# Raw weights of the second and third expert fetched one stage earlier, in a fused four-layer kernel

## The reference

```python
x = layernorm(x + dilated_attention(x))        # 16 heads, segments of 256, every second row
x = layernorm(x + expert_layer(x))             # below
x = layernorm(x + linear_attention(x, W))
x = layernorm(x + soft_moe(x, phi, W, b))

# expert_layer, x as 4096 rows of 256
route = softmax(x @ router_w + router_b)
for e in range(8):
    a, g = split(x @ w1[e])                    # w1[e]: 256 x 2048
    y = (silu(a) * g) @ w2[e]                  # w2[e]: 1024 x 256
    out = where(argmax(route) == e, y, out)
out = out * max(route)
```

## Time and profile before

| | us |
|---|---|
| median of 3 runs | 1556.09 (1555.97 to 1556.95) |
| the profiled execution | 1556.61 |
| its span, first to last instruction | 1554.6 |
| TensorE busy in the span | 1387.7 (89%) |
| VectorE, ScalarE, POOL busy | 885.5, 611.6, 672.0 |

### The profile page before, as it was taken

The page is one execution under the profiler, slowest core; times in us unless marked ns, Lnnn a source line. Parts: engine busy times, 40 slices in busy tenths (PEclk is TensorE's granted clock), DMA queues, the critical chain, the costliest instruction groups (busy, mean ns, idle before and its releaser), DMA issues. The chain is left out here.

```text
span 1554.6 us, 27807 instructions
## 1 busy us (share of the span) xinstructions
PE 1387.7 (89%) x8930; PEld 1206.6 (78%) x8931; DVE 885.5 (57%) x1771; ACT 611.6 (39%) x1076; POOL 672.0 (43%) x542
## 2 busy tenths in 40 slices
PE   6997397999999993799969999999999968999997
PEld 3444276888888882577769999999999958989997
DVE  4788522222222223367578787787787734565555
ACT  3554332333333332476543332332332315555553
POOL 6663087776660005211017665565565523150400
PEclk9998688999999996799989999999999988999999
DMA  4112333222220005300032265365366367355440
GB/s 156 45 44 87 111 121 103 95 96 105 96 81 13 13 14 203 95 1 1 1 118 85 82 176 154 102 175 167 93 182 169 92 177 281 127 213 203 149 149 27
DMA packets 109178, 171.17 MB, mean 110 GB/s; under 512 B 6112, under 2 KB 95072, under 8 KB 101696
## 3 DMA queue, kind: packets, MB, share of 16 engines
q1 hardware_dynamic: 100096, 156.00, 31.2%
q0 software_dynamic: 3408, 9.31, 2.1%
q10 hardware_dynamic: 5616, 5.11, 1.0%
HBM read 114.96 MB, written 55.44 MB: 110 GB/s over the span
## 5 line engine op out<-in xcount | busy, mean ns | idle before, releaser
L1492 PE MATMUL disp_psS<-disp_e,last_x 128*128 128x256 f32 x1024 | 233.1, 381 | 3.8 <-POOL disp_e L1575 3.8
L1492 PEld LDWEIGHTS disp_psS<-disp_e,last_x 128*128 128x128 f32 x1024 | 191.1, 191 | 28.5 <-POOL disp_e L1575 4.4
L1582 POOL TENSOR_TENSOR disp_s<-disp_e 128x512 f32<-128x512 f32 x64 | 82.3, 1286 | 262.9 <-ACT disp_e L1562 262.9
L1761 PE MATMUL comb_psO<-comb_yh,comb_eh 128*128 (+1 forms) x512 | 156.6, 306 | 15.3 <-DVE comb_el L1852 11.6
L1544 ACT ACTIVATE disp_raw<-disp_psL 128x512 f32<-128x512 f32 x128 | 76.4, 597 | 220.5 <-PE disp_psL L1477 155.7
L1477 PE MATMUL disp_psL<-phi_hi,disp_xh 128*128 (+1 forms) x512 | 156.9, 306 | 4.9 <-DVE disp_e L1638 4.8
L1575 POOL TENSOR_TENSOR disp_e<-disp_e,disp_rs 128x1024 f32<-128x1024 f32 x64 | 151.7, 2371 | 0.0
L1852 DVE TENSOR_TENSOR comb_el<-comb_psT,comb_eh 128x512 fp32r<-128x512 f32 x128 | 86.7, 687 | 106.4 <-ACT comb_eh L1797 106.4
L1477 PE MATMUL disp_psL<-phi_hi,disp_xl 128*128 (+1 forms) x512 | 145.6, 284 | 0.0
L1477 PE MATMUL disp_psL<-phi_lo,disp_xh 128*128 (+1 forms) x512 | 145.6, 284 | 0.0
L1761 PE MATMUL comb_psO<-comb_yl,comb_eh 128*128 (+1 forms) x512 | 145.5, 284 | 0.0
(11 more groups left out here) (261 smaller groups left out, 3437.1 us busy)
## 6 DMA issues: line engine op xcount, KB each, us to landing
logits<-disp_raw SPq DMA_DIRECT2D x64, 512.0 KB, 4.1
comb_e<-logits SPq DMA_DIRECT2D x32, 1024.0 KB, 4.9
w_raw<-in_w SPq DMA_DIRECT2D x8, 2048.0 KB
disp_wt<-in_w_slot SPq DMA_DIRECT2D x16, 1024.0 KB, 8.1
w_raw<-in_w SPq DMA_DIRECT2D x8, 1024.0 KB
disp_bt<-in_b_slot SPq DMA_DIRECT2D x8, 1024.0 KB, 11.3
comb_y_in<-slot_y SPq DMA_DIRECT2D x4, 2048.0 KB, 10.4
slot_y<-disp_yb SPq DMA_DIRECT2D x60, 128.0 KB, 2.8
```

Of the source, the lines that this page charges most:

```text
L1492: last = nc.tensor.matmul(psS[kd][:, b, :], x[:, b * TB + mc, kd * P:(kd + 1) * P], e[mc % 4][:, b, :], start=mc == 0 and b % 2 == 0, stop ...
L1582: nc.gpsimd.tensor_tensor(s2[:], e[mc % 4][:, 0:2, :], e[mc % 4][:, 2:4, :], ALU.add).then_inc(pair_sum, 1)
L1761: last = nc.tensor.matmul(psO[j % 2][:, 0:D], ep[s % EB][:, i, :], yp[:, bass.ds(odd, 1), ch * D:(ch + 1) * D].rearrange("p a d -> p (a d) ...
```

## The change

Expert 1's raw weights get a place of their own, `next1` and `next2`. It is not new memory: it lies over the second place of `lo1` and `lo2`, which is filled first by expert 1's own low part. `low_chunk` therefore reads a chunk and writes its low part to the same bytes. SP loads expert 1 in the attention, after the loads of segments 2 and 3, once expert 0 has landed. The second pair of segments is written out ahead of the loop, which now begins at 2. In the routing SP loads expert 2 into `raw1` and `raw2`, which are free since expert 0 has been split. In the experts SP's loads begin with expert 3, and its wait for eight gathers is gone.

```diff
--- before.py
+++ after.py
@@ -72,6 +72,10 @@
 
     def sb(self, name, shape, dt=F32):
         return self.ctx.enter_context(self.nc.sbuf_tensor(f"{self.tag}_{name}", shape, dt))
+
+    def over(self, name, shape, offset):
+
+        return self.nc.alloc_sbuf_tensor_at(f"{self.tag}_{name}", shape, F32, offset=offset)
 
     def ps(self, name, shape, dt=F32):
         return self.ctx.enter_context(self.nc.psum_tensor(f"{self.tag}_{name}", shape, dt))
@@ -213,13 +217,15 @@
                 wait(sp, loaded, i * 16)
                 sp.dma_start(dst[:, bass.ds(segs[0], 2), :], src[:, bass.ds(segs[0], 2), :]).then_inc(loaded, 16)
                 for q in range(2):
-                    if not isinstance(i, int):
+                    if not isinstance(i, int) or i > 0:
                         sp.wait_ge(xT_raw, i * 2 + (q - 1))
                     sp.dma_start(xe[q][:], src[:, bass.ds(segs[q], 1), 0:D].rearrange("p a d -> p (a d)")).then_inc(even_loaded[q], 16)
 
             load(0, (0, 1))
             weights.load(sp, 0)
-            with sp.Fori(1, NSEG // 2) as i:
+            load(1, (2, 3))
+            weights.load(sp, 1)
+            with sp.Fori(2, NSEG // 2) as i:
                 load(i, (sp.snap(i * 2), sp.snap(i * 2 + 1)))
 
         @block.gpsimd
@@ -558,7 +564,7 @@
             sp.wait_ge(rw_clear, 1)
             sp.dma_start(rw[:, :, 0:NE], router_w.rearrange("(k p) e -> p k e", p=P)).then_inc(w_loaded, 16)
             sp.dma_start(rb[:], router_b.partition_broadcast(P)).then_inc(w_loaded, 16)
-            weights.load(sp, 1)
+            weights.load(sp, 2)
             for b in range(B):
                 sp.wait_ge(kept, (b + 1) * TB)
                 sp.dma_start(x1_dram.rearrange("(t p) d -> p t d", p=P)[:, b * TB:(b + 1) * TB, :],
@@ -741,9 +747,13 @@
         self.raw1 = m.sb("raw1", [P, KD, 2 * FF])
         self.raw2 = m.sb("raw2", [P, FK, D])
         self.hi1 = m.sb("hi1", [P, 2, KD * 2 * FF], F32R)
+        lo1_at = nc.sbuf_base
         self.lo1 = m.sb("lo1", [P, 2, KD * 2 * FF], F32R)
         self.hi2 = m.sb("hi2", [P, 2, FK * D], F32R)
+        lo2_at = nc.sbuf_base
         self.lo2 = m.sb("lo2", [P, 2, FK * D], F32R)
+        self.next1 = m.over("next1", [P, KD, 2 * FF], lo1_at + 4 * KD * 2 * FF)
+        self.next2 = m.over("next2", [P, FK, D], lo2_at + 4 * FK * D)
         self.zero = m.sb("zero", [P, 1])
         self.loaded1, self.loaded2, self.zeroed = m.sem("loaded1"), m.sem("loaded2"), m.sem("zeroed")
 
@@ -751,9 +761,14 @@
 
     def load(self, sp, e):
 
-        wait(sp, self.split, 4 * e)
-        sp.dma_start(self.raw1[:], self.w1_dram[e].rearrange("(k p) f -> p k f", p=P)).then_inc(self.loaded1, 16)
-        sp.dma_start(self.raw2[:], self.w2_dram[e].rearrange("(k p) d -> p k d", p=P)).then_inc(self.loaded2, 16)
+        raw1, raw2 = (self.next1, self.next2) if e == 1 else (self.raw1, self.raw2)
+        if e in (1, 2):
+            sp.wait_ge(self.loaded1, 16 * e)
+            sp.wait_ge(self.loaded2, 16 * e)
+        if e > 1:
+            sp.wait_ge(self.split, 4 if e == 2 else 4 * e)
+        sp.dma_start(raw1[:], self.w1_dram[e].rearrange("(k p) f -> p k f", p=P)).then_inc(self.loaded1, 16)
+        sp.dma_start(raw2[:], self.w2_dram[e].rearrange("(k p) d -> p k d", p=P)).then_inc(self.loaded2, 16)
 
     def high_slice(self, act, seg, ready):
 
@@ -778,7 +793,7 @@
 
     def divide_high(self, act, e):
 
-        for loaded, raw, hi, _ in self.parts():
+        for (loaded, _, hi, _), raw in zip(self.parts(), (self.next1, self.next2)):
             act.wait_ge(loaded, 16 * (e + 1))
             self.nc.scalar.activation(hi[:, e, :], raw[:].rearrange("p k f -> p (k f)"), ACT.Copy).then_inc(self.high, 1)
 
@@ -789,7 +804,8 @@
 
         first = KD * 2 * FF // self.CHUNK
         part, at = (0, n) if n < first else (1, n - first)
-        _, raw, hi, lo = self.parts()[part]
+        _, _, hi, lo = self.parts()[part]
+        raw = (self.next1, self.next2)[part]
         cols = slice(at * self.CHUNK, (at + 1) * self.CHUNK)
         pool.wait_ge(self.high, 2 * (e - 1) + part + 1)
         last = self.nc.gpsimd.tensor_tensor(lo[:, e, cols], raw[:].rearrange("p k f -> p (k f)")[:, cols], hi[:, e, cols].bitcast(F32),
@@ -858,9 +874,7 @@
 
         @block.sync
         def _(sp):
-            for q in range(4):
-                sp.wait_ge(gathered[q], 32)
-            for e in range(2, NE):
+            for e in range(3, NE):
                 w.load(sp, e)
 
         @block.gpsimd
```

## The result

The changed kernel takes 1568.4 us (median; 1564.37 to 1572.17), the kernel before 1556.32 us, ten runs each: ratio 1.0073, 95% interval [1.0056, 1.0091]. It is 12.1 us slower; a gain of 5.3 us was forecast. The profiled execution is 1566.82 us, its span 1565.0.

What follows compares the result with a forecast made beforehand. One chain of stages bounds the kernel, with TensorE setting the end of the experts. Hole -5.3, attention 0 and routing 0 sum to -5.3 us: 1551.3 us profiled, 1550.8 us median, range 1542 to 1559.5.

Steps and rivals of the forecast that it cites:

- Attention and routing at nothing: Stages before the experts: the moved loads of experts 1 and 2 cost 0 us; attention 2.8 us if transfers took twice as long.
- POOL's two waits go, last gather at 252: Experts: waits of 3.47 and 2.40 us before two gathers vanish, 5.3 us net; last gather at 252.1 instead of 257.34.
- The division starts at 254.1: Experts: POOL's division of expert 2 starts at 254.1 instead of 259.35 us, worth nothing by itself.
- The failed step: Experts: TensorE's slow stretch still begins at 248.07 but ends with the gathers, shrinking from 13.3 to 8.0 us.
- the hole: Experts, kernel before: TensorE's matmuls crawl without a releaser from 248 to about 261.3 us, costing 12.5 us in one tile.
- The other half of the step: Experts: TensorE's slow stretch ends when the last gathered rows land, at about 255.9 us after the change.
- the term of -5.3 us: Experts: the gain from shortening the hole, the only nonzero term; shorter hole given 0.34.
- The prediction's own sign of being wrong: Experts: wrong if the slow stretch keeps 13 us, is absent, starts before 245, or TensorE waits for a split.
- The rival "Slower": Experts: a long unbroken run of gathers makes the hole, then 232.8 to 256 us; 1566 us, chance 0.20.
- the +10: Experts: the slower rival's added cost, a hole of 23.3 us instead of 13.3.
- a late supply of instructions to TensorE: Experts: rival's cause; without the transfer of 223.22 the hole goes, 13.1 us gained, 1543.0 us, chance 0.24.

Runs made afterwards that it cites:

- e3: Changed kernel with expert 2's 3 MB transferred once more at 223 us, its division waiting for the repeat: 1554.1 us, 0.9996 of the kernel before.
- e8: Kernel before, 15 expert gathers in a row, the other 24 one at a time between POOL's divisions of experts 2 to 7: 1539.29 us, ratio 0.989.
- e1: Changed kernel, 15 expert gathers in a row, the other 24 one at a time between POOL's divisions of experts 2 to 7: 1537.17 us, ratio 0.9878.
- e2: Kernel before with expert 2's load held until all 39 gathers have landed: 1566.35 us, ratio 1.0075.
- e13: Changed kernel with a 1.3 us POOL subtraction after the 23rd and 31st expert gather alone: 1560.25 us, 1.0031 of the kernel before.
- e5: Changed kernel with a 128x512 POOL subtraction after each expert gather from the sixteenth on: 1569.03 us, 1.008 of the kernel before.
- e15: Changed kernel with 24 expert gathers placed singly between POOL's divisions, the kernel of e1 run again: 1540.75 us, 0.9907 of the kernel before.
- e12: The changed kernel itself, run again unaltered on one chip with three variants: 1565.97 us, 1.0072 of the kernel before.
- e9: Kernel of e1 plus a POOL subtraction after each linear-attention gather from the ninth on: 1548.65 us, 1.0117 of the kernel before.
- e11: Changed kernel with a 128x512 POOL subtraction after the 23rd and 31st expert gather alone: 1526.68 us, 0.998 of the kernel before.

## Why the prediction was wrong

**Attention and routing at nothing: right.** The routing begins at 143.40 us (143.41 before), and e3, with both early loads and the old transfer, takes the time of the kernel before (0.9996); e8 against e1 agrees.

**POOL's two waits go, last gather at 252: right**, to 0.3 us.

**The division starts at 254.1: wrong by 2.4 us**; it waited for TensorE's signal of the fourth tile, which came with the end of the stream. Nobody waited for it.

**The failed step is the onset of the hole.** The prediction says that it begins "at a place of TensorE's program which the change leaves where it is, at 248.07". It begins some 10 us after the gathers start to come every 1.25 us, wherever TensorE then is: at 232.9 instead of 248.5 us, in another tile and among other matmuls. e3 brought the brake back and the late hole with it, e2 took the brake from the kernel before and got the early one. The other half of the step, that it ends when the gathers have landed, held (255.5 and 256.5 us). With the wrong onset the term of -5.3 us had the wrong sign; measured it is +14.0: the change took away the transfer that had kept half of the hole shut. The prediction's own sign of being wrong, a slow stretch that starts before 245, is what the profile shows.

**The rival "Slower" was right** in place and size: 232.8 to 256 us forecast, 232.9 to 256.5 seen, 1566 against 1568.4 us. Its mechanism was right in that the run of gathers makes the hole; that the run must be unbroken is what e13 refutes, and the +10 was too small by 4 us: it did not have TensorE's wait of 15.15 us for VectorE, which itself waited for a late signal. I gave it 0.20 because TensorE ran evenly in the earlier run of gathers and in the loaded stretch. Both have an answer that stood in the rows: from 190 to 223 us a chunk of POOL work stands between two gathers (2.4 us apart), and up to 238 us the transfer slowed them. In both stretches they were not dense, and the loaded one was not wholly undisturbed: ScalarE's "remote" waits of 2.54 us before 229.12 and 4.20 before 237.45 lie in it. "Nothing else marks the onset" should have weighed more than "TensorE's place did not change", which was no evidence at all: a place in the program explains a slow stretch only if something there is slow.

**What the prediction left out:** the waits of other engines in the hole. ScalarE's "remote" waits in the trace of before would have shown that TensorE's signals are late as well, which a late supply of instructions to TensorE does not explain, and the same waits in the linear attention would have shown a second place with dense gathers and the same sign.

**Open:** by what path gathers hold up TensorE; whether their rate counts or the number in flight; and why one batch of runs does not show it. There the changed kernel itself was not run.

## What to carry to other kernels

Before a transfer is moved away, ask what it slowed down: a brake on another queue can be worth more than the bandwidth it takes. When an engine crawls without a releaser, list what starts about then and what ends with it on every other engine, and weigh the onset as much as the end. Try indirect gathers from GpSimd spaced to 1.6 to 2 us each (by waiting for the second one before, or by putting them between long POOL operations) rather than issued back to back, watch who waits for the last of them (e5 lost 25.1 us there), and time it on more than one chip.

## What the runs showed of the hardware that was not expected

- Gathers of 128 rows issued from GpSimd every 1.25 us delay TensorE: its semaphore increments are 4 us late 9 us after they begin and up to 26 us later on, and from some 10 us on its instructions come 0.7 us or more apart. At 1.35 us on the mean four fifths of it remain, at 1.6 us in the experts and 1.99 us in the linear attention nothing; half the bytes change nothing. The Trainium skill, "SBUF — State Buffer", section Who interferes with whom, holds that a DMA never contends with a compute engine. Taken for the time of a kernel, the measurement says otherwise for these gathers (e15 against e12, on one chip: 25.2 us); no run shows whether SBUF has a part in it.
- The cost is not always there: in one batch of three kernels (e9 to e11), on a chip where nothing else was run, the traces show neither the hole nor the waits, and the kernel before ran in 1529.94 us instead of 1555 to 1556. The four other batches of experiments, on three chips, all had it.
- A POOL subtraction with two inputs from SBUF stretched VectorE's operations with two inputs from 0.17 us to 1.75 us (e9 against e11).
